# Routed experts in steps of 128 slots with resident weights and tokens held in TensorE; context kept in DRAM for the last layer; one ring of three banks in both attention cores

## The reference

```python
x = x + tanh(g_xattn[0]) * L0_xattn(layernorm(x), ctx, ...)   # softmax attention, 496 keys + 16 extra keys ("dca")
x = x + tanh(g_ffn[0])   * L0_ffn(layernorm(x), ...)
x = x + tanh(g_xattn[1]) * L1_xattn(...);  x = x + tanh(g_ffn[1]) * L1_ffn(...)
x = x + tanh(g_xattn[2]) * L2_xattn(ctx, layernorm(x), ...)   # state-space scan
x = x + tanh(g_ffn[2])   * L2_ffn(layernorm(x), ...)          # 8 experts, top 2, silu-gated, inner 352
x = x + tanh(g_xattn[3]) * L3_xattn(layernorm(x), ctx, positions, ...)  # softmax attention with rope
x = x + tanh(g_ffn[3])   * L3_ffn(layernorm(x), ...)          # 2 shared + 16 routed experts, top 2, gelu, inner 256
```

```python
probs = softmax(xt @ W_router); top_v, top_i = top_k(probs, 2)
routed = sum over the two experts of top_v * (gelu(x @ Wrt_up[e]) @ Wrt_down[e])
```

## Time and profile before

| quantity | value |
|---|---|
| median of 3 runs | 3214.14 us (3209.91 to 3215.42) |
| profiled execution | 3215.47 us, its span 3213.7 us |
| mean granted TensorE clock | 0.90 |
| busy in the span | PE 77%, DVE 68%, ACT 50%, PEld 37%, POOL 35% |
| attention core, layer 0 | about 236 to 566 us |
| gated routed steps, 8 experts | 1808 to 2118 us, read-back to 2172 |
| attention core, layer 3 | about 2338 to 2757 us |
| routed steps, 16 experts | 2957 to 3158 us, read-back to the end |

### The profile page before, as it was taken

One profiled execution on the slowest core, in us unless ns is written; L12 is line 12 of the kernel. 1 busy time (PEld: TensorE's weight loads), 2 busy tenths in 40 slices (PEclk: granted clock), 3 DMA queues, 4 the chain that ended last, 5 costly groups with the idle time before them and its releaser, 6 DMA issues. The chain is left out here.

```text
span 3213.7 us, 40834 instructions
## 1 busy us (share of the span) xinstructions
PE 2476.1 (77%) x14030; PEld 1185.7 (37%) x14030; DVE 2175.4 (68%) x3403; ACT 1615.9 (50%) x2278; POOL 1121.1 (35%) x807
## 2 busy tenths in 40 slices
PE   2987889799969935676675599937878899797993
PEld 1541333344434311222223477724512222354661
DVE  6655764435357798999996666655578888546664
ACT  2543555154432665555542355535546767433873
POOL 5764666002001235666662222145541000001444
PEclk9987999899979967899886799978979999998996
DMA  3532220230000000000001577743622100212997
GB/s 126 197 151 72 83 83 15 82 112 1 1 4 12 1 0 1 0 0 1 0 0 53 181 241 240 234 131 124 224 99 80 47 21 14 99 47 99 325 305 238
DMA packets 161699, 300.70 MB, mean 94 GB/s; under 512 B 33540, under 2 KB 79376, under 8 KB 159623
## 3 DMA queue, kind: packets, MB, share of 16 engines
q1 hardware_dynamic: 138646, 219.23, 19.6%
q0 software_dynamic: 22896, 79.44, 8.3%
HBM read 206.08 MB, written 92.27 MB: 93 GB/s over the span
## 5 line engine op out<-in xcount | busy, mean ns | idle before, releaser
L1817 DVE TENSOR_REDUCE ac_nmax<-ac_M 128x1 f32<-128x512 f32 (+1 forms) x768 | 496.6, 687 | 148.7 <-PE ac_M L1631 144.3
L1795 ACT ACTIVATE ac_PT<-ac_S 128x1024 f32<-128x1024 f32 x384 | 371.1, 1017 | 158.7 <-PE ac_S L1666 138.9
L3370 POOL TENSOR_TENSOR sc_hc<-sc_h,sc_cs 128x1024 f32<-128x1024 f32 x128 | 300.7, 2357 | 160.4 <-DVE sc_h L3485 96.4
L3485 DVE TENSOR_TENSOR_SCAN sc_h<-sc_dA,sc_dB 128x1024 f32<-128x1024 f32 x128 | 292.1, 2282 | 12.7 <-ACT sc_dA L3451 12.7
L3405 PE MATMUL sc_y<-sc_hc,ident 128*128 128x512 f32 x512 | 258.1, 631 | 18.3 <-DVE x_res L3501 16.1
L3451 ACT ACTIVATE sc_dA<-ss_delta,sc_A 128x511 f32<-128x511 f32 x256 | 166.0, 682 | 29.9 <-DVE sc_h L3485 29.3
L3383 PE MATMUL sc_b<-ss_bc,sc_sel 128*128 128x512 f16 x128 | 54.1, 423 | 156.4 <-DVE sc_dB L3477 124.9
L1631 PE MATMUL ac_M<-KT,QT 64*128 64x512 f16 (+1 forms) x384 | 141.5, 429 | 41.3 <-DVE ac_nmax L1817 24.6
L3456 ACT ACTIVATE sc_cs<-sc_c 128x512 f32<-128x512 f32 x128 | 76.3, 596 | 185.6 <-POOL sc_hc L3370 182.5
L3477 DVE TENSOR_TENSOR sc_dB<-ss_du,sc_b 128x1024 f32<-128x1024 f32 x128 | 156.1, 1220 | 18.9 <-PE sc_b L3383 7.5
L730 DVE SCALAR_TENSOR_TENSOR mo_up16l<-mo_up,mo_up16h 128x1408 f16<-128x1408 f32 (+1 forms) x77 | 112.7, 1464 | 64.0 <-ACT mo_up16h L670 63.9
(11 more groups left out here) (610 smaller groups left out, 6010.5 us busy)
## 6 DMA issues: line engine op xcount, KB each, us to landing
keys_t<-ap_kto SPq DMA_DIRECT2D x32, 512.0 KB, 2.6
queries_t<-ap_qto SPq DMA_DIRECT2D x32, 512.0 KB, 2.7
mo_up<-in_w_gate SPq DMA_DIRECT2D x23, 704.0 KB, 5.1
mo_up<-in_w_up SPq DMA_DIRECT2D x23, 704.0 KB, 6.7
mo_up<-in_exp_up SPq DMA_DIRECT2D x31, 512.0 KB, 6.1
mo_dn<-in_exp_down SPq DMA_DIRECT2D x31, 512.0 KB, 7.5
slot_results_last<-mo_o SPq DMA_DIRECT2D x31, 512.0 KB, 6.0
mo_dn<-in_w_down SPq DMA_DIRECT2D x23, 512.0 KB, 7.1
```

The source lines that it names most:

```text
L1795: nc.scalar.activation(PT[:, n % PTB, :, :], psS[:, 2 * (n % 2):2 * (n % 2) + 2, :], ACT.Exp, scale=SCALE / (SQK * SQK)).then_inc(exp_done, 1)
L1817: last = v.tensor_reduce(out[:, :, 0], sc[:, 0:MAIN], AX.X, ALU.max)
L3370: nc.gpsimd.tensor_tensor(hc[:, m % RC, :, :], h[:, m % RH, :, :], cs[:, m % 2, :].unsqueeze(1).to_broadcast([P, W, S]), ALU.mult).then_in ...
L3485: nc.vector.tensor_tensor_scan(h[:, m % RH, :, :].rearrange("p c s -> p (c s)"), dA[:, m % 2, :, :].rearrange("p c s -> p (c s)"), dB[:, m ...
```

## The change

- **Routed block.** `SLOTS` becomes 128: 39 steps in layer 2 and 47 in layer 3, every expert having at least one. The split weights of all experts are kept in SBUF. Step s, for s below the number of experts, belongs to expert s, and during it expert s + 1 is split and expert s + 2 loaded by constant address, through a ring of 3 (gated) or 5 stage pieces. Later steps load no weights.
- TensorE reads the expert number itself, `expert_of(s)` and `expert_of(s - 1)` in each step. The up products now hold the tokens (128 columns) and stream the weights (352 or 256 columns) addressed by the register; the middle comes out with slots on the partitions, is activated in one go, and is turned by 3 or 2 transposes before the down products. The step's order on TensorE is: rows of step s + 1 turned, first pass of up, middle of step s - 1 turned, other two passes, down products of step s - 1.
- POOL gathers two steps ahead instead of one; the read-back uses the stage's memory, with 4 tiles in the gated block.
- **Context.** Its split halves are written to DRAM in layer 0's weights block, freed after layer 2's attention part, and loaded again in layer 3's weights block; `project_k` waits for them batch by batch.
- **Attention cores.** `psM` becomes a ring of three banks and `px` is gone: maxima, rows, dca and sums products and turned tiles all take their place in the ring. The copies of the dca and sums banks go from ACT to DVE. `scores_t(n + 3)` comes after `more(n)`.

The core of the diff:

```diff
-SLOTS = 256
+SLOTS = 128
...
         def run_steps(engine, step):
-            for s in range(2):
-                step(s, s, s < 1, s < 2, False)
-            with engine.Fori(1, (NS - 2) // 2) as i:
...
+            for s in range(n_exp):
+                step(s, s % 2)
+            with engine.Fori(n_exp // 2, (NS - TAIL) // 2) as i:
+                step(i * 2, 0)
+                step(i * 2 + 1, 1)
...
         def _(sp):
-                e = sp.value_load(step_expert[0:1, bass.ds(s, 1)], min_val=0, max_val=w_down.shape[0] - 1)
...
+            def load(e, i):
+                q = e * NPC + i
+                if q >= NST:
+                    sp.wait_ge(w_ready, pieces_split(q - NST))
+                if i < n_up:
+                    src = [w_up[i][first_expert + e].rearrange("(k p) i -> p k i", p=P)]
...
         def _(pe):
+            def expert_of(s):
+                return pe.value_load(step_expert[0:1, bass.ds(s, 1)], min_val=0, max_val=n_exp - 1)
...
+            def up(s, w, e, some):
+                for i in some:
+                    a, h = passes[i]
                     for k in range(KD):
...
+                        for j in range(n_up):
+                            last = nc.tensor.matmul(pu[w][:, j, 0:inner], y16[a][:, w, k, :], up16[h][:, bass.ds(e, 1), j, k, :],
+                                                    start=(i == 0 and k == 0), stop=(i == 2 and k == KD - 1))
...
+            def down(s, w, e):
...
+                for c, n in enumerate(chunks):
+                    for a, b in passes:
+                        last = nc.tensor.matmul(po[w][:], mid16[a][0:n, w, c, :], dn16[b][0:n, bass.ds(e, 1), c, :],
+                                                start=(i == 0), stop=(i == len(passes) * NC - 1))
...
+            def step(s, w):
+                e = expert_of(s)
+                before = expert_of(s - 1) if from_step(s, 1) else None
+                if before_end(s, 1):
+                    rows_transposed(s + 1, 1 - w)
...
+                up(s, w, e, (0,))
+                if from_step(s, 1):
+                    middle_transposed(s - 1, 1 - w)
+                up(s, w, e, (1, 2))
+                if from_step(s, 1):
+                    down(s - 1, 1 - w, before)
...
         def _(act):
...
+            def step(s, w):
+                more = filling(s) and s + 1 < n_exp
+                if from_step(s, 2):
+                    results(s - 2, w)
+                if before_end(s, 1):
+                    y_high(s + 1, 1 - w)
+                if from_step(s, 1):
+                    middle_high(s - 1, 1 - w)
+                if more:
+                    weights_high(s + 1, (0,))
+                first_half(s, w)
+                if more:
+                    weights_high(s + 1, range(1, NPC))
...
+            for b in range(B):
+                for tile, kept in zip((env.ctx_hi, env.ctx_lo), env.ctx_d):
+                    a, c = tile[:, :, b * S:(b + 1) * S], kept[:, :, b * S:(b + 1) * S]
+                    if rope:
+                        sp.dma_start(a, c).then_inc(w["ctx_in"][b], 16)
+                    else:
+                        sp.dma_start(c, a).then_inc(ctx_out, 16)
...
-        psS, psM, po, px = ps("S", [P, 4, S]), ps("M", [P, 2, S]), ps("o", [P, S]), ps("x", [P, S])
+        psS, psM, po = ps("S", [P, 4, S]), ps("M", [P, NRING, S]), ps("o", [P, S])
...
         for i, x in enumerate(use):
-            ring[x] = (i % 2, use[i - 2] if i >= 2 else None)
+            ring[x] = (i % NRING, use[i - NRING] if i >= NRING else None)
...
                 scores_t(n + 2)
-                scores_t(n + 3)
                 if g and s == 3 and not rope:
                     turned(g - 1, 1)
                 more(n)
+                scores_t(n + 3)
                 values(n + 1)
                 more(n + 1)
...
-                if not rope:
-                    nc.scalar.activation(oT[:, 1, :], px[:], ACT.Copy).then_inc(d_ev, 1)
...
+            def dca_out(g):
+                dve.wait_ge(dca_mm, g + 1)
+                if g:
+                    dve.wait_ge(ot_T, 3 * g)
+                v.tensor_copy(oT[:, 1, :], bank_of("dca", g)).then_inc(d_ev, 1)
```

More of the change, by code:

```diff
@@ L495, in routed_block @@
[L495 to L500, removed]
+        up16 = [sb(f"up16{h}", [P, n_exp, n_up, KD, inner], F16) for h in "hl"]
+        dn16 = [sb(f"dn16{h}", [P, n_exp, NC, D], F16) for h in "hl"]
+        stage = sb("stage", [P, NST, PIECE])
@@ new lines, in staged, with arrivals, pieces_split @@
+        def staged(e, i):
+            s = stage[:, (e * NPC + i) % NST, :]
+            if i < n_up:
+                return [s[:, 0:KD * inner].rearrange("p (k n) -> p k n", k=KD)]
+            s = s[:, 0:NC * D].rearrange("p (c n) -> p c n", c=NC)
+            return [s[:, 0:full, :]] + ([s[0:rest, full, :]] if rest else [])
+        def arrivals(q):
+            return 16 * sum(operations(p % NPC) for p in range(q % NST, q + 1, NST))
+        def pieces_split(q):
+            return sum(operations(p % NPC) for p in range(q + 1))
@@ L550, in step @@
[L550 to L554, removed]
-            def store(s, w):
[L557 to L560, removed]
+            def load(e, i):
+                q = e * NPC + i
+                if q >= NST:
+                    sp.wait_ge(w_ready, pieces_split(q - NST))
+                if i < n_up:
+                    src = [w_up[i][first_expert + e].rearrange("(k p) i -> p k i", p=P)]
+                else:
+                    src = [w_down[first_expert + e, 0:full * P, :].rearrange("(c p) n -> p c n", p=P)]
+                    src += [w_down[first_expert + e, full * P:inner, :]] if rest else []
+                for a, b in zip(staged(e, i), src):
+                    sp.dma_start(a, b).then_inc(w_in[q % NST], 16)
@@ L751, in step @@
-            def step(s, w, first, early, last):
-                if not last:
-                    y_low(s + 1, 1 - w)
-                for c in range(NC):
-                    chunk(s, w, c)
-                    if not last and c < n_up:
-                        up_low(s + 1, 1 - w, c)
-                if not last:
-                    down_low(s + 1, 1 - w)
+                nc.vector.scalar_tensor_tensor(out=y16[1][:, w, :, :], in0=pT[:], scalar=SY, in1=y16[0][:, w, :, :],
+                                               op0=ALU.mult, op1=ALU.subtract).then_inc(yl_done, 1)
@@ L873, in _ @@
             sp.wait_ge(small_in, 16 * n)
+            if not rope:
+                sp.wait_ge(ctx_out, 16 * 2 * B)
         @block.gpsimd
```

510 lines of the change are left out of this document (271 added, 239 removed).

## The result

The changed kernel takes 3193.0 us (3192.0 to 3200.3, 5 runs) against 3213.3 (5 runs): ratio 0.9943, interval 0.9928 to 0.9957. The direction was right, the size a quarter of the forecast: 3193.0 lies in the stated range of 3065 to 3235, and outside the forecast's own band of 3080 to 3160.

| stage | before | after | difference | forecast |
|---|---|---|---|---|
| attention core, layer 0 | 331.6 | 318.8 | −12.8 | −24 |
| gated routed block | 374.6 | 360.1 | −14.5 | −35 |
| attention core, layer 3 | 423.8 | 407.8 | −16.0 | −42 |
| routed block, 16 experts | 270.9 | 300.8 | +29.8 | +14 |
| all else (two projections −4.0, scan −3.5, router −2.2, late block +0.8) | | | −9 | +1 |

The account below looks back on a forecast made before the run. Routed stretches were taken as array-bound before, attention cores as held by TensorE and DVE trading banks. Cores −66, routed −20, around them −2 and context +3 gave −85 from 3215.5: 3130 us, range 3065 to 3235.

Parts of the forecast that it names:

- the sequencer's terms: TensorE's sequencer in routed steps: operands, pushes, value reads and waits, 6.0 us a gated step, 4.4 a last-layer one.
- a third score bank, no extra bank: Attention cores: waits between TensorE and DVE shrink, saving 42 us in the last layer's core and 24 in the first's.
- The copies moved to DVE: First layer's core: two copies from ACT, 0.69 us each, bring DVE to 13.5 us a group, under TensorE's 16.3.
- Rival 2: Attention cores: ordered maxima, shared products in the ring and DVE's copies limit the gain to 15 us; 3180 us, chance 0.11.
- Operand and push: Routed steps, TensorE's sequencer: 0.10 us per register-addressed matmul operand, plus 0.026 us to push each matmul.
- Waits and their counts: Routed steps, TensorE's sequencer: about 8 waits with counts at 0.05 us, 0.4 us a step.
- The two reads: Routed steps, TensorE's sequencer: two expert numbers read per step, 1.2 us gated and 1.6 us last layer.
- a slack of 10 us: Gated routed stretch: 10 us added because array, ring and sequencer do not cover each other exactly.
- The filling steps: Gated block while experts load: 8.8 us an expert, 2.5 over the array, 17 us over 7 steps.
- Rival 1: Routed steps: register operands cost TensorE's sequencer far more, losing from P = 0.15; about 3308 us at 0.20; chance 0.17.
- milder form: Routed steps: register operand cost P from 0.12 to 0.15 us, total 3160 to 3215 us; chance 0.16.
- The signs that I named: Matmul starts, sequencer rows, step and group times; wrong if last routed block under 190 or over 260 us, or group 12.5.

Follow-up runs that it names:

- the fastest kernel: The change with old order of second score products, one expert read per step, routed steps written out and no bounds check: 3086.9 us, ratio 0.9617.

## Why the prediction was wrong

Of the missing 65 us, 37 are in the cores, 20 in the gated block, 16 in the last, 73 in all; about 10 came back elsewhere (−9 for a forecast of +1). Those 9 have no cause shown: such stages moved by up to 3.5 us between kernels that do not differ there (the scan took 506.0 us before and 502.5 with only the attention core changed).

Two steps failed: the move of `scores_t(n + 3)` stood in no term of the sum (37 us), and the sequencer's terms were too small (36 us over both routed blocks, with the first loads of the gated one).

- **Attention cores: −66 forecast, −29 measured.** The step that failed: "a third score bank, no extra bank" was priced, and the move of `scores_t(n + 3)` behind `more(n)` not at all, though it stood in the diff. The priced part was right: 1.3 and 1.5 us a group forecast (−42 and −24), 1.27 and 1.42 measured with the old order (−41.3 and −25.4). TensorE's busy time was a good floor in the last core and in the first. The copies moved to DVE show no cost, as said: the first core made its forecast with them, though no run takes them apart. The price of the move is 25 us in the last core and 12 in the first. Rival 2 (rings give little) came near the size (a gain of 15 for 29), but its mechanism, turned tiles in the ring, was not the cause: they stay in the ring in the old order, which gains the whole 67.
- **Last routed block: +14 forecast, +29.8 measured.** The bound was named rightly and mis-sized: 4.4 us a step against 5.22. Operand and push: 0.126 forecast, 0.134 measured. Waits and their counts: 0.4 forecast, about 0.9 measured, as instructions of 0.05 us follow each other at 0.1. The two reads were taken from SP's rows at 1.6 and took 1.44. The 16 steps without a loop took 4.7. Loop end: left out, 0.25 a step, though the trace of before had the row of TensorE's branch, here in the gated steps (min, median and max in ns):

```profile
L517 PEldq COMPARE_BRANCH  x9: 76/213/236, 1856.0 to 2069.8; - x9
```

- **Gated block: −35 forecast, −14.5 measured.** The same three terms, over 33 operands, and the two reads, 1.2 forecast from SP's rows and 1.42 measured: 6.0 forecast, 7.08 measured, and so above the array's 6.29, which I had right to 0.01. I had put a slack of 10 us where a new bound of 0.8 us a step stood. With one read taken away (steps of 6.34) the block is 34 us under before, the forecast. The filling steps (8.8 forecast) took 9.1 on average from the third to the eighth, and the second took 14.9, which I had not foreseen.
- **Rival 1** had the mechanism. Its P counts the operand without the push: 0.107 measured, near the 0.10 I took and below its milder form; the losing side, P from 0.15, was not reached. The blocks became as dear as in the milder form by waits and loop ends, and that the total fell among its 3160 to 3215 us is luck: half of the miss is in the cores. Its break-even takes 22 us off for drains, landings and slack, its case at P = 0.20 only 12; with 12 in both it is 0.157.
- **Context, router, read-back:** within 3 us of what was said.
- **The signs that I named** would not have found it. The last block's steps took 237 us, inside 190 to 260; a last-core group took 12.0, not 12.5. The 352-column matmuls still start 0.149 us apart, the array's pace, since an operand costs the sequencer 0.134: it falls behind on waits, reads and the loop's end, and the place to look is the idle time before the step's first transpose.

What stays open: what the 0.1 us from one short instruction to the next is made of, why a filling step of the gated block stays 0.7 us over the loop's, and the second one 2.5, when loads are small, and whether maxima could be spread without splitting the four heads.

## What to carry to other kernels

Price every moved line of a hand-written order: an instruction put behind a wait on an in-order engine costs its full time once per turn (0.22 us here, four times a group). When a matmul's address comes from a register, count 0.13 us of sequencer for it and 0.7 us for each value read, as measured here, and take distances between instructions, not their durations. Reading once, writing steps out and dropping the check brought the gated steps to the array's 6.29 us and the last ones to 3.97, 0.24 above what they take without registers. Two edits in one change should be run one at a time: here one undid 37 of the other's 67 us.

## What the runs showed of the hardware

- The branch at a loop's end lasts 0.22 us on TensorE's sequencer (x13 in the change's last block); on DVE, ACT, POOL and SP it lasts 0.045 to 0.063.
- Four float32 matmuls that hold 32 columns each take together about what one takes; two and two take about twice that (106 us for 784 records, 175 for 664).
- Register instructions of 0.055 us duration are 0.134 us apart with a matmul between.
- A value read takes TensorE's sequencer 0.66 us in the kernel with one read a step, and 0.36 us without the bounds check in the fastest kernel.
